# Last slot: batch 15's group norm and output product ahead of batch 14's LayerNorm, and unread products in TensorE's gaps

## The reference

```
x = x + 0.5 * ffn0(layernorm(x))                 # int4-rounded kernel + low-rank term, bias
x = x + retention0(layernorm(x))                 # 8 heads, decay, group norm, gate, output product
x = x + 0.5 * ffn0(layernorm(x))
x = x + 0.5 * mod(layernorm(x))
x = x + retention1(layernorm(x))                 # 4 heads, RMS norm per head, gate, output product
x = x + 0.5 * mod(layernorm(x))

def mod(h):                                      # L1_ffn
    scores = einsum('bsd,d->bs', h, w_router)
    top_scores, top_idx = top_k(scores, 256)     # 256 of 512 tokens of each batch
    processed = gelu(h[top] @ W1 + b1) @ W2 + b2
    return h with sigmoid(top_scores) * processed added at top_idx
```

## Time and profile before

| what | value |
| --- | --- |
| median of 3 runs | 805.19 us (804.76 to 806.33) |
| the profiled execution | 807.99 us |
| its span, first to last instruction | 805.8 us |
| TensorE busy (matmuls / weight loads) | 757.8 / 614.8 us |
| VectorE busy | 665.8 us |
| GpSimd busy | 475.3 us |
| ScalarE busy | 424.5 us |
| mean granted TensorE clock | 0.977 of 2.4 GHz |

### The profile page before, as it was taken

One profiled execution on the slowest core, in us unless ns is written; L12 is line 12 of the kernel. 1 busy time (PEld: TensorE's weight loads), 2 busy tenths in 40 slices (PEclk: granted clock), 3 DMA queues, 4 the chain that ended last, 5 costly groups with the idle time before them and its releaser, 6 DMA issues.

```text
span 805.8 us, 29577 instructions
## 1 busy us (share of the span) xinstructions
PE 757.8 (94%) x13001; PEld 614.8 (76%) x13001; DVE 665.8 (83%) x1825; ACT 424.5 (53%) x875; POOL 475.3 (59%) x375
## 2 busy tenths in 40 slices
PE   5778999999999999998999999999999999999875
PEld 4666888787887787776878888877888888878653
DVE  6686888888888999997858889987777988888887
ACT  2333555565555565654554446655544565564745
POOL 4467888887888888876543444444434344453544
PEclk9996999999999999999999999999999999999988
DMA  7000100011111110010000000000000000000113
GB/s 229 30 28 29 29 28 16 16 28 29 29 28 30 28 29 2 3 55 3 1 2 2 3 3 2 2 2 2 3 2 2 3 2 2 3 2 16 55 39 105
DMA packets 23284, 18.57 MB, mean 23 GB/s; under 512 B 2146, under 2 KB 20468, under 8 KB 22900
## 3 DMA queue, kind: packets, MB, share of 16 engines
q1 hardware_dynamic: 22596, 16.40, 7.0%
q10 hardware_dynamic: 560, 0.28, 0.1%
HBM read 12.48 MB, written 4.19 MB: 21 GB/s over the span
## 4 chain that ended last, share of the span: by engine, by line
PE 75%; DVE 17%; POOL 3%; ACT 2%; issue 1%; DMA 0%; DVEq 0%; POOLq 0%; ACTq 0%
PE ps L286 20%; PE ps L410 11%; PE ps L401 10%; PE ps L281 5%; PE ps L675 4%; PE ps L364 3%; PE ps L308 3%; PE ps L297 3%; PE ps L384 3%; PE ps L394 2%; POOL grstd L1067 2%; PE ps L356 2%; DVE x L1225 2%; PE ps L667 2%; PE ps L320 2%; PE ps L685 2%
## 5 line engine op out<-in xcount | busy, mean ns | idle before, releaser
L1067 POOL TENSOR_TENSOR grstd<-gve,mhalf 128x32 f32<-128x32 f32 (+1 forms) x32 | 159.0, 4968 | 26.5 <-DVE gve L1280 26.5
L410 PEld LDWEIGHTS ps<-w_s,hid 128*128 128x128 f32 x1024 | 123.5, 192 | 9.0 <-issue 8.0
L410 PE MATMUL ps<-w_s,hid 128*128 128x128 f32 x1024 | 129.0, 277 | 0.7 <-issue 0.7
L401 PE MATMUL ps<-xt_r,w_s 128*128 128x512 f32 x256 | 126.7, 617 | 0.7 <-ACT xt_r L822 0.7
L826 ACT ACTIVATE hid<-ps,b_s 128x512 f32<-128x512 f32 x128 | 84.0, 726 | 24.0 <-PE ps L401 23.8
L1063 POOL TENSOR_TENSOR r_ret<-ve_ret,powers 128x8 f32<-128x8 f32 x32 | 57.8, 1807 | 27.6 <-DVE ve_ret L1211 27.6
L286 PE MATMUL ps<-w_qkvg,xt_p 128*128 128x128 f32 x512 | 71.2, 285 | 2.8 <-ACT xt_p L822 2.8
L1073 POOL TENSOR_TENSOR um<-um 128x96 f32<-128x96 f32 (+1 forms) x32 | 21.3, 665 | 88.5 <-DVE um L1259 88.5
L401 PEld LDWEIGHTS ps<-xt_r,w_s 128*128 128x128 f32 x256 | 45.2, 192 | 35.1 <-issue 30.1
L1058 POOL TENSOR_TENSOR rstd_ln_mod<-ve_ln_mod,mhalf 128x4 f32<-128x4 f32 x32 | 32.3, 1010 | 65.3 <-DVE ve_ln_mod L1211 65.3
L1253 DVE TENSOR_TENSOR sc<-ps,tri 128x1024 f32<-128x1024 f32 (+1 forms) x64 | 58.3, 953 | 15.1 <-PE ps L320 7.6
(11 more groups left out here) (236 smaller groups left out, 1749.8 us busy)
## 6 DMA issues: line engine op xcount, KB each, us to landing
xtin<-in_xt SPq DMA_DIRECT2D x16, 256.0 KB, 3.8
out_x<-base SPq DMA_DIRECT2D x16, 256.0 KB, 2.3
xin<-in_x SPq DMA_DIRECT2D x15, 256.0 KB, 3.0
rot<-in_rot SPq DMA_DIRECT2D x2, 1024.0 KB, 5.9
w_s<-in_w SPq DMA_DIRECT2D x2, 256.0 KB
xin<-in_x ACTq DMA_DIRECT2D x1, 256.0 KB, 4.0
w_qkvg<-in_wqkvg SPq DMA_DIRECT2D x1, 256.0 KB, 3.8
w_qkv<-in_wqkv SPq DMA_DIRECT2D x1, 256.0 KB
```

The lines of the kernel that those rows point to most:

```text
L401: nc.tensor.matmul(bank(k), w1_s[:, f, :], xt["r"][:].rearrange("p j n -> p (j n)"), start=True, stop=True).then_inc(s[f"h{f}"], 1)
L410: mm = nc.tensor.matmul(bank(k, j * P, P), hid[:, f, j * P:(j + 1) * P], w2_s[:, f, :], start=False, stop=(f == last and j == NT - 1), ski ...
L1067: nc.gpsimd.tensor_tensor(grstd[:, 0:n], gve[:, 0:n], mhalf[:, 0:n], ALU.pow) \
```

## The change

Nearly all of it is in `slot_end`. After batch 15's attention products, its group norm, gate and output product now go ahead of batch 14's LayerNorm and feed-forward part on all engines, and are done in two token halves: TensorE transposes and ScalarE squares a half, VectorE sums it, GpSimd takes the root of 8 columns per half. The product with the gate comes before the root is applied. One half product of batch 14's output goes ahead of the attention products. Batch 15's residual sum goes into `x2b`, so that `x2` stays for batch 14. VectorE's `keep_base` becomes `scaled_base` on ScalarE, with weights from `base_weights`. The group mask is made by small matmuls with selectors (`group_mask`, `group_weigh`) in place of transposes, and the four tie-settling steps get shorter. `mod` results of batches 14 and 15 are no longer copied from PSUM: ScalarE scales batch 14's in its bank, and VectorE reads batch 15's there. `keep_busy` puts in matmuls that nobody reads: 14 in `slot_end`, 5 in the first slot. `prepare_rest` makes two more selectors.

```diff
@@ TensorE @@
+            def keep_busy(times, k):
+                for _ in range(times):
+                    nc.tensor.matmul(bank(k, 0, P), ident, ident, start=True, stop=True)
+            def group_mask(src, to, k, first):
+                for j in range(NT):
+                    mm = nc.tensor.matmul(bank(k, GB * j, GB), src[:, j * P:(j + 1) * P], to,
                                           start=(first and j == 0), stop=not first, skip_group_check=True)
...
                         routed_up(3, up[3])
                     routed_up(2, up[2])
+                if g < 0:
+                    keep_busy(5, 2)
...
+            def gated_half(half):
+                wait(pe, "gy_half", half + 1)
...
+            def output_half(half):
+                wait(pe, "gt_half", half + 1)
...
                 rank_sum(3, 0, 1)
+                output_b(old, (2,))
                 for c in range(NT):
                     attend_b(c, c == NT - 1, sl)
-                output_b(old, (2, 3))
+                output_b(old, (3,))
                 rank_sum(3, 1, 1)
-                transpose_y(now)
+                wait(pe, "ycopy", now)
+                for half in range(2):
...
+                    mm.then_inc(s["y_half"], 1)
+                keep_busy(14, X1)
+                gated_half(0)
+                gated_half(1)
+                output_half(0)
+                output_half(1)
+                rank_sum(3, 2, 1)
                 wait(pe, "ln_mod_xn", old)
...
                 wait(pe, "ln_mod_xt", now)
                 last_rows(NB - 1, YB)
-                rank_mask(3, YB + 1)
+                wait(pe, "k_over", 1)
+                group_mask(msk_a, sel_f[:], 2, True)
+                wait(pe, "k_mask", 4)
+                group_mask(picked, sel_l[:], 2, False).then_inc(s["k_mt"], 1)
                 last_column(NB - 1, 0)
                 wait(pe, "act2", old)
                 routed_up(0, X1)
+                last_sum(0, 1)
                 wait(pe, "act3", old)
                 routed_up(1, 3)
-                last_sum(0, 1)
...
-                wait(pe, "ystore", old)
+                wait(pe, "k_bank", 4 * (ROUNDS + 2))
                 routed_down(0, 2, now)
@@ ScalarE @@
+            def scaled_base(b, src, n, count):
+                wait(act, "base_w", n + 1)
+                for j in range(NT):
+                    last = nc.scalar.activation(base[:, b * S + j * P:b * S + (j + 1) * P], src[:, j, :], ACT.Identity,
+                                                bias=base_w[:, n, 1, j:j + 1], scale=base_w[:, n, 0, j:j + 1])
+                last.then_inc(s["base"], 1)
...
                 weigh(5)
-                wait(act, "ytok", now)
-                nc.scalar.activation(sq[:], PS[:, YB * BANK:(YB + 2) * BANK], ACT.Square).then_inc(s["sq"], 1)
+                for half in range(2):
+                    wait(act, "y_half", half + 1)
+                    nc.scalar.activation(sq[:, half * S:(half + 1) * S], bank(YB + half), ACT.Square) \
+                        .then_inc(s["sq_half"], 1)
                 weigh(6)
+                copy_half(0)
+                copy_half(1)
                 normalise(old)
...
-            weigh(LAST, "weighted")
+            wait(act, "mod", 2 * NB - 1)
+            for j in range(NT):
+                y = bank(YB + 1, j * P, P)
+                ins = nc.scalar.activation(y, y, ACT.Copy, scale=wcol[:, LAST * NT + j:LAST * NT + j + 1])
+            ins.then_inc(s["weighted"], 1)
@@ GpSimd @@
                 for n in range(3):
                     add_output(n)
+                for half in range(2):
+                    at = slice(2 * half * H1, 2 * (half + 1) * H1)
+                    wait(pool, "gve_half", half + 1)
+                    nc.gpsimd.tensor_tensor(grstd[:, at], gve[:, at], mhalf[:, at], ALU.pow).then_inc(s["grstd_half"], 1)
                 root("ln_mod", old)
-                group_root(4 * H1, now)
-                wait(pool, "gy", now)
+                wait(pool, "gy_half", 2)
                 for n in range(3, 6):
                     add_output(n)
+                wait(pool, "ln_mod_xn", old)
                 root("ln_mod", now)
@@ VectorE @@
+                half_sums(0, sl)
+                half_sums(1, sl)
+                for half in range(2):
+                    at = slice(half * S, (half + 1) * S)
+                    wait(dve, "sq_half", half + 1)
+                    nc.vector.tensor_tensor(t2[:, at], bank(YB + half), gate[sl.buf(0)][:, at], ALU.mult) \
+                        .then_inc(s["yg"], 1)
+                normed_half(0)
                 variance("ln_mod", x2, ve["ln_mod"], old)
-                head_sums(H1, V1, sl)
-                negative_mean(old)
+                normed_half(1)
                 rank_narrow(3, 1, 1)
                 rank_try(2)
...
-                output(NB - 1)
+                wait(dve, "mod", 2 * NB)
+                for j in range(NT):
...
-                nc.vector.tensor_tensor(base[:, at], base[:, at], yall[:, at], ALU.add).then_inc(s["out_dve"], 1)
+                nc.vector.tensor_tensor(base[:, at], bank(YB + 1), base[:, at], ALU.add).then_inc(s["out_dve"], 1)
```

123 lines of the change are left out of this document (89 added, 34 removed).

## The result

| | before | after |
|---|---|---|
| median of three runs | 805.19 us (804.76 to 806.33) | 815.88 us (815.37 to 817.35) |
| profiled execution, its own time | 807.99 us | 815.37 us |
| its span | 805.8 us | 813.3 us |
| ratio of the times | | 1.0133, 95% interval 1.0098 to 1.0168 |

The account below looks back on a forecast made before the run. The kernel was taken as bound by TensorE through its slots, its end set by one sequence on VectorE. Terms +1.1 +6.6 +1.9 +0.7 -0.4 = +9.9 us, added to the median 805.19, gave 815.1 us; range 809.5 to 819.

Parts of the forecast that it names:

- The block: Last slot, GpSimd: batch 15's root waits behind batch 7's add, so batch 15's mean comes 1.1 us later.
- The queue behind it: Last slot: rank tries 4 and 5, then TensorE's work, follow batch 15's mean; mean to search grows by 6.6 us.
- TensorE's queue of 7.5 us: Last slot: matmuls queued on TensorE from the end of rank try 5 to the search's start, 7.5 us.
- The lead of the product: Last slot: batch 15's output product, moved ahead, reaches VectorE 5.4 us earlier.
- The clock: Last slot, TensorE: a new gap of 6.2 us halves the clock from 785.0 to 789.9, +1.9 us.
- Search to end: Last slot: GpSimd's last add ends 15.5 us after the search's first maximum, not 14.8, +0.7 us; the end follows 4.5 later.
- The start: First slot: five unread matmuls hidden in TensorE's idle time keep up some of the clock, -0.4 us.
- Adding to the median: Whole kernel: the terms, as differences, were added to the median 805.19 us, not to the profiled 807.99 us.
- The block that costs nothing: Rival, last slot: batch 15's root runs when its variance is ready; +2.3 us, 807.5 us; chance 5%.
- The whole lead: Rival, last slot: the search moves forward by the product's full 5.4 us, 799.8 us; chance 4%.
- The start did not decide: Rival denied here, first slots: avoiding all three half-clock stretches returns 10.1 us, 805.4 us, no change; chance 3%.
- The first norm half did not wait for the second root: Rival denied here, last slot: VectorE's first norm half waits for GpSimd's second root, +0.7 us, 815.8 us; chance 10%.

Follow-up runs that it names:

- Experiment 1: The changed kernel with ScalarE's scaling of batch 7 moved from behind batch 14's third activation to behind the scaling of batch 6: 809.3 us, ratio 1.0034.
- Experiment 2: The changed kernel with rank tries 4 and 5 put ahead of batch 15's negative mean on VectorE: 809.1 us, ratio 1.0031.
- experiment 3: The changed kernel with both batch 7's scaling early on ScalarE and rank tries 4 and 5 ahead of batch 15's mean on VectorE: ratio 1.0042.
- rebuilt versions: Three reorderings of the changed kernel: early product kept, batch 7's scaling, rank tries and batch 13's store earlier, adds placed differently in each: ratios 1.0025, 0.9990, 0.9961.
- Experiment 4: The changed kernel with GpSimd's roots of batches 14 and 15 ahead of the adds of batches 5, 6 and 7: 812.3 us, ratio 1.0076.
- experiments 1 and 5: The second of the two: the changed kernel with 24 unread matmuls on TensorE between batch 14's third up matmul and rank sum 4: ratio 1.0115.
- last two versions: The changed kernel reordered, with GpSimd's adds of batches 5 to 7 held until both base weights, or until the selection steps end: ratios 0.9990 and 0.9961.
- experiment 7: The kernel before with only the five unread matmuls in the first slot added: ratio 0.9984, interval 0.9966 to 1.0002.
- the last version: The changed kernel reordered on four engines, GpSimd's adds of batches 5 to 7 moved into the search: 803.7 us, ratio 0.9961 to the kernel before.
- the version before it: The changed kernel reordered on four engines, GpSimd's adds of batches 5 to 7 waiting for both base weights: ratio 0.9990 to the kernel before.

## Why the prediction held, and where its steps were off

**The block: right.** The forecast named the add for batch 7, behind ScalarE's scaling, behind batch 14's third activation. GpSimd idled 8.82 us in front of it ("about 8"), and VectorE 6.39 us ("some 6"). Experiment 1 removed it and brought back 5.6 of the 10.9 us in its profile, and some 8 by the ratios.

**The queue behind it: right, and the main term.** Mean to search grew by 7.6 us (4.5 to 12.1); the forecast had 6.6 and 1.9 for the clock, 8.5. Experiment 2 shows it alone, experiment 3 that TensorE's queue of 7.5 us is in it as forecast.

**The lead of the product: mis-sized.** 5.4 us were forecast, 3.6 came (31.7 to 28.1 behind the mark). Three parts: the copy of y came 0.9 us later than before, not 0.55; the clock was half from 766.6 to 770.0, which the forecast priced at nothing and bounded at 0.75 to 3, and the second gated half and the eight output products took 1.3 us more than in the rebuilt versions (1.11 and 3.05 us against 0.66 and 2.2); small waits the rest. Part of it is chance of this profile: in six others with the same code up to there the copy came 0.5 us later than before, and VectorE took up the product at 27.6 to 27.8, a lead of 4.0. The late product made rank try 3 end 1.75 us later than forecast, and from there to the mean it took 6.4 us, as forecast. So it alone makes the mean's +2.8 in place of +1.1.

**What was not in the sum: adds beside VectorE.** Batch 14's mean took 0.80 us and not 0.16, beside the add of 767.61; the mean at 781.29, with no add beside it, took 0.17. It delayed batch 14's up matmuls by 0.6 us, but in the changed kernel that cost nothing: TensorE idled 1.86 us between them and rank sum 3 (774.96), waiting for try 3. Experiment 4 took the adds away from there, and the product was not earlier (27.8). The missing term cost something only in the versions where an add ran beside batch 15's mean or the selection.

**Luck in the total.** In the last slot 1.7 us too little for the mean, 0.9 too much for mean to search and 0.2 too much for the way to the last add leave 0.6 us, 10.9 against 10.3. The sum came closer than its terms.

**The clock: the size was near, its place was not sure.** The gap was 6.05 us (6.2 forecast) and the clock half from 780.4 to 787.2, in which TensorE worked for 4.2 us (4.9 forecast). Filling it gave 1.2 us, of 1.9. In the forecast the clock's loss was a fixed part of a path. In experiments 1 and 5 a fall that was gone at one place came at another; in 2 and 3 no second fall came, and in the last two versions none in the slot until its last matmul was done.

**Search to end: right.** 15.3 us to GpSimd's last add, 15.5 forecast; 4.6 us from there to the end, 4.5 forecast. The DMA was full as forecast, from 810 to 812 (shares of 1.02 and 1.03, before 1.04). The four output steps that read PSUM took 1.13 us (1.15 forecast).

**The start:** 0.4 us were forecast, experiment 7 gives 0.16% or 1.3 us with an interval of -0.2 to 2.7.

**Adding to the median: it served, with some luck.** Added to the profiled 807.99 us the terms would have given 817.9. The profiled execution of the kernel before had a mean clock of 0.977; of the 23 later runs on one chip the two at 0.976 took 808.1 us, and the seven at 0.987 or 0.988 took 801.6 to 805.8. There is no trace of a median run, and its last slot may differ by the 2 us of experiment 7.

**The rivals.** The block that costs nothing is out. Its price, 807.5 us for a mean that comes on time, is near the 807.9 us (1.0034) of experiment 1, but not for its reasons: it had the search at 41.8 behind the mark, and the profile of experiment 1 has it at 45.1. The whole lead did not arrive, though the last version shows that a search before 40.3 can be had, only with another order on TensorE, VectorE, ScalarE and GpSimd. The start did not decide (experiment 7). The first norm half did not wait for the second root: it began at 763.96 as soon as its factors were there and took 0.68 us inside that root (762.12, two of 1.63). But the mechanism behind that rival is at work elsewhere in this slot, between adds and VectorE's steps, where I had not looked.

## What to carry to other kernels

When work is moved ahead, walk every in-order queue once more from the new arrival times: the step that costs is the one whose place in a queue did not matter while its input was late, and then what is queued behind it counts more than the wait itself. A step of 0.16 us on the critical path can take 1.2 beside another engine's elementwise add; put such adds where VectorE reads PSUM or waits anyway. Before a longer step is blamed, look for slack behind it: 0.6 us here cost nothing. Unread matmuls need their own run before they are believed.

## What the runs showed of the hardware

VectorE and GpSimd shut each other out in this kernel, instruction by instruction. A step on batch 14's mean took 0.80 us beside the add of 767.61 and ended with it; the mean of batch 15 took 1.09 or 1.10 beside another, a sum of two 128x1 values 1.18, the scan 2.17 and not 1.28. The other way round an add took 1.73 and not 1.27 behind a VectorE step that had begun first, and a root of 4 columns took 1.40 and not 1.02 beside the second norm half (766.24). Steps with an operand in PSUM kept their time beside the same adds. So did some with one SBUF input: two of one value in each partition took 0.15 and 0.16 us (781.32 and 783.34 in the last version), and the comparison of a 128x512 tile took its 0.75 (777.66 in the version before it). The Trainium skill (SBUF — State Buffer, "Who interferes with whom") states this as a lock: a VectorE instruction with two SBUF inputs and a GpSimd instruction that reads SBUF block each other, and the first to issue wins. The rows of the adds agree. The base weight, a scalar step with one SBUF input, took 1.20 (768.93); the page names such steps too, in their fast mode, and no row shows in which mode this one ran.

The same page would have the first norm half wait for the second root, a GpSimd instruction that reads SBUF. Here the row disagrees: 0.68 us, inside a root of 1.63. As far as these rows go, a root of few columns that has started lets a VectorE step pass, and one that is issued beside such a step is late.

The clock: a last slot of the same code had 6.8 us of half clock in one profile and 10.2 in another. With 24 unread matmuls in the longest gap the fall came 13 us later, after 7 us of work without a gap. In the three rebuilt versions, with 8 more unread matmuls, TensorE idled 0.35 and 0.36 us ahead of the two gated halves in place of 1.02 and 1.48, and the fall at 766 did not come; but these versions differ in more than that. No run here shows what decides the place.
